# Loads in quarters, and the first group's projections, statistics and norm inside the context phase

## What is computed

```python
x = x + attn(layernorm(x))            # 16 heads of 32, causal
x = x + xattn(layernorm(x), ctx)      # below
x = x + ffn(layernorm(x))             # 8 experts of width 1024, top-p routing

# xattn: 16 heads of 128 in 8 groups; fp8_linear rounds its input to fp8 after a division by a scale
q,  k, v = ln(fp8_linear(h, wq)),  ln(fp8_linear(h, wk)), fp8_linear(h, wv)
core     = gqa(q, k, v)                            # two heads of a group share k and v
qx       = ln(fp8_linear(h, wqx))
kx, vx   = ln(ctx @ wkx), ctx @ wvx
xout     = gqa(qx, kx, vx)
return fp8(cat(core, xout) / smooth) @ wproj * scales
```

## Time and profile before

| what | value |
|---|---|
| three runs | 2502.35, 2497.77, 2496.59 us; median 2497.77 |
| the profiled execution | 2499.1 us, span 2497.3 us, mean granted clock of PE 0.967 |
| PE busy | 2314.2 us, 93% of the span |
| DVE, ACT, POOL busy | 57%, 46%, 46% |
| context phase, prologue, steps, experts (start, about) | 310, 533, 565, 1475 us |
| ACT's loads, landing in the median | w_group 5.1 us (1 MB, x15), w_kv 7.5 us (0.5 MB, x7), kv 6.5 us (1 MB, x16) |

### The profile page before, as it was taken

The page is one execution under the profiler, slowest core; times in us unless marked ns, Lnnn a source line. Parts: engine busy times, 40 slices in busy tenths (PEclk is TensorE's granted clock), DMA queues, the critical chain, the costliest instruction groups (busy, mean ns, idle before and its releaser), DMA issues. The chain is left out here.

```text
span 2497.3 us, 39715 instructions
## 1 busy us (share of the span) xinstructions
PE 2314.2 (93%) x14528; PEld 1305.7 (52%) x14528; DVE 1417.8 (57%) x2920; ACT 1139.2 (46%) x2165; POOL 1150.0 (46%) x1412
## 2 busy tenths in 40 slices
PE   6899798958999989999999849999999999999999
PEld 3566544435666666666666534444444444444444
DVE  5766786327999989899999853222222222222221
ACT  3455475438777878777778721111111111111110
POOL 3422346647787878677775423131313131313131
PEclk9799899979999999999999969999999999999999
DMA  4100022217877787878878742111111111111000
GB/s 150 35 19 18 3 83 85 102 68 154 160 143 155 166 167 138 171 154 157 155 144 166 130 136 101 40 62 44 57 46 54 50 50 54 47 58 43 0 0 34
DMA packets 421569, 224.80 MB, mean 90 GB/s; under 512 B 404400, under 2 KB 404912, under 8 KB 413232
## 3 DMA queue, kind: packets, MB, share of 16 engines
q1 hardware_dynamic: 415952, 186.74, 32.5%
q10 hardware_dynamic: 5472, 36.18, 4.3%
HBM read 103.34 MB, written 18.87 MB: 49 GB/s over the span
## 5 line engine op out<-in xcount | busy, mean ns | idle before, releaser
L1835 ACT ACTIVATE sil<-bank 128x512 f32<-128x512 f32 x128 | 76.4, 597 | 772.5 <-PE bank L299 772.5
L1808 POOL TENSOR_SCALAR hh<-h 128x512 f16<-128x512 f32 x128 | 104.8, 819 | 680.8 <-DVE h L1906 680.8
L1906 DVE TENSOR_TENSOR h<-bank,sil 128x512 f32<-128x512 f32 x128 | 88.6, 692 | 530.6 <-PE bank L299 423.1
L1450 ACT ACTIVATE xprob<-bank,xnm 128x1024 f32<-128x1024 f32 (+1 forms) x240 | 219.9, 916 | 184.1 <-DVE xnm L1538 183.7
L1538 DVE TENSOR_REDUCE xnm<-bank 128x1 f32<-128x512 f32 (+1 forms) x256 | 243.2, 950 | 67.7 <-PE bank L299 66.0
L1550 DVE SCALAR_TENSOR_TENSOR xparts<-xprob,xri,xparts 128x1024 f16<-128x1024 f32 (+1 forms) x240 | 278.3, 1160 | 4.4 <-ACT xparts L1458 4.2
L1458 ACT ACTIVATE xparts<-xprob,xri 128x1024 f16<-128x1024 f32 (+1 forms) x240 | 227.5, 948 | 4.6 <-DMA xpt<-xparts 4.5
L297 PE MATMUL bank<-eXTh,ewh_gate 128*128 128x512 f16 x512 | 194.8, 380 | 3.5 <-DVE ewl_gate L1853 3.5
L298 PE MATMUL bank<-eXTh,ewl_gate 128*128 128x512 f16 x512 | 194.8, 380 | 0.0
L299 PE MATMUL bank<-eXTl,ewh_gate 128*128 128x512 f16 x512 | 194.7, 380 | 0.0
L297 PE MATMUL bank<-eXTh,ewh_up 128*128 128x512 f16 x512 | 194.1, 379 | 0.0
(11 more groups left out here) (264 smaller groups left out, 5949.8 us busy)
## 6 DMA issues: line engine op xcount, KB each, us to landing
xkv<-kv_made ACTq DMA_DIRECT2D x16, 1024.0 KB, 6.5
raw_gate<-in_gate SPq DMA_DIRECT2D x8, 2048.0 KB, 7.9
raw_up<-in_up SPq DMA_DIRECT2D x8, 2048.0 KB, 8.0
raw_down<-in_down SPq DMA_DIRECT2D x8, 2048.0 KB, 7.7
xwraw<-in_w_group ACTq DMA_DIRECT2D x15, 1024.0 KB, 5.1
kv_made<-vst SPq DMA_DIRECT2D x16, 512.0 KB, 4.3
kv_made<-kst SPq DMA_DIRECT2D x16, 512.0 KB, 2.6
kvraw<-in_w_kvx SPq DMA_DIRECT2D x4, 1024.0 KB, 6.4
```

Of the source, the lines that this page charges most:

```text
L1450: act.activation(prob[prob_of(u)][:, 0:L], SC[u % 2][:, 0:L], ACT.Exp, bias=nm[:, u % 4:u % 4 + 1], accum_out=rs[:, u % 4:u % 4 + 1]).then ...
L1808: pool.tensor_scalar(hh[half][:, f, :], h[i % 2][:], 1.0, 1.0, ALU.mult, ALU.mult).then_inc(h_hi, 1)
L1835: act.activation(sil[i % 2][:], bank[:, 2 * (i % 2), :], ACT.Silu, scale=1.0 / WS).then_inc(silu, 1)
L1906: dve.tensor_tensor(h[i % 2][:], bank[:, 2 * (i % 2) + 1, :], sil[i % 2][:], ALU.mult).then_inc(made, 1)
```

## The change

- The buffer of the projected blocks, `qr`, and the value parts of batch 0, `v0`, are allocated before `second_norm` and handed to both phases.
- In the context loop PE runs the six jobs A0 to A3, B0, B1 of step 0 at iterations 31, 33, 35, 37, 39 and 41 (`first_job`), in the free banks 0 and 1. ACT reads them one iteration later (`first_read`), DVE makes their low part and statistics two iterations later (`first_low`). POOL makes rstd and shift ahead of its `deviations(5)` (`first_deviations`) and waits for the result. ACT applies them to the four key blocks at iteration 55, DVE to 16 blocks in iterations 54 to 61, two in each.
- `total` is no buffer of its own any more: DVE writes y + unit over y, and so ACT waits for `r_out`, the end of the last subtraction, before it fills y again. The statistics of the first jobs lie in `unit`. Chain buffers are shared.
- The prologue of the group stage keeps only T_ORDER = T4 T0 T1 T2 T3; counts on semaphores are lowered to match.
- Each load of the group stage becomes four transfers, each a quarter of every partition's row: kv in slots 6 to 9 of both batches, w3 in slots 10 to 13 of b = 0, w2 two by two in slots 4 and 5 of b = 0, w1 of group g + 2 in slots 10 to 13 of b = 1, and w1 of group 1 in slots 0 to 3 of step 0. The first kv load, ahead of the steps, is also in four.

```diff
+FIRST_FROM, FIRST_EVERY = 31, 2
 def second_norm(...):
+    FIRST = ("A0", "A1", "A2", "A3", "B0", "B1")
+    def first_at(i):
+        return [(i - FIRST_FROM) // FIRST_EVERY] if (i >= FIRST_FROM and (i - FIRST_FROM) % FIRST_EVERY == 0
+                                                     and (i - FIRST_FROM) // FIRST_EVERY < len(FIRST)) else []
...
             for q in range(BATCHES):
+                if q == BATCHES - 3:
+                    first_deviations()
+                    pool.wait_ge(f_shift, 1)
                 deviations(q)
...
-                    act.wait_ge(r_dve, ROUND_STEPS * (j - 1))
+                    act.wait_ge(r_out, j - 1)
...
                 read(i)
+                for f in first_at(i - 1):
+                    first_read(f)
+                if i == 55:
+                    act.wait_ge(f_shift, 1)
+                    for k in ACT_APPLIES:
+                        act.activation(first_block(k), first_block(k), ACT.Identity, scale=frstd[:, k:k + 1],
+                                       bias=fshift[:, k:k + 1])
...
-                round_fp8(dve, r_dve, ROUND_STEPS * j, y[j % 2][:], unit[:], total[:])
+                round_fp8(dve, r_dve, ROUND_STEPS * j, y[j % 2][:], unit[:], y[j % 2][:])
...
+                for f in first_at(i - 2):
+                    first_low(f)
+                if 54 <= i < 62:
+                    dve.wait_ge(f_shift, 1)
+                    for k in (2 * (i - 54), 2 * (i - 54) + 1):
+                        dve.tensor_scalar(first_block(k), first_block(k), frstd[:, k:k + 1], fshift[:, k:k + 1],
+                                          ALU.mult, ALU.add)
...
+            def first_job(f):
+                if f == 0:
+                    pe.wait_ge(L_f, B * KT)
+                    pe.wait_ge(r_out, B * KT)
+                if name[0] == "A" and f >= 2:
+                    pe.wait_ge(f_read, f - 1)
...
             for i in range(CROSS):
                 project(i)
+                for f in first_at(i):
+                    first_job(f)
                 for j in norms_at(i):
                     turn_norm(j)
...
 def group_attention(...):
-            deviations(0)
-            apply(0)
             for name in T_ORDER:
                 turned_lo(name, 0, 0)
...
-                    act.dma_start(wraw[:], ins["w_group"][bass.ds(g, 1), chunk // 2].rearrange("a p k n -> p (a k) n"))\
-                        .then_inc(w_in, 16)
+                    act.dma_start(wraw[:, k, :], ins["w_group"][g, chunk // 2, :, k, :]).then_inc(w_in, 16)
...
-            for name in NEXT:
-                if name == "T4":
-                    apply_keys(0)
+            for name in T_ORDER:
                 read_job(name, 0, 0)
...
-                    if b == 0:
-                        if u == 0 and not last_group:
-                            load(1, g + 1, w_base(g))
-                            load(2, g + 1, w_base(g))
-                        if u == 8:
-                            load(3, g, w_base(g) + (W1N if not last_group else 0))
-                            load_kv(g, 1, PAIRS * n)
-                    if b == 1 and u == 8 and not last_group:
-                        load_kv(g + 1, 0, PAIRS * n)
+                    if n == 0 and u < KT:
+                        load(1, 1, 0, u)
+                    if b == 1 and 10 <= u < 10 + KT and g + 2 < GROUPS:
+                        load(1, g + 2, w_base(g + 1), u - 10)
+                    if b == 0 and 6 <= u < 6 + KT:
+                        load_kv(g, 1, PAIRS * n, u - 6)
+                    if b == 0 and 10 <= u < 10 + KT:
+                        load(3, g, w_base(g) + (W1N if not last_group else 0), u - 10)
+                    if b == 1 and 6 <= u < 6 + KT and not last_group:
+                        load_kv(g + 1, 0, PAIRS * n, u - 6)
+                    if b == 0 and u in (4, 5) and not last_group:
+                        for k in (2 * u - 8, 2 * u - 7):
+                            load(2, g + 1, w_base(g), k)
...
-            for name in NEXT:
-                run_job(name, 0, 0, NEXT, ())
+            for name in T_ORDER:
+                run_job(name, 0, 0, T_ORDER, ())
```

## The result

| | before | after |
|---|---|---|
| median of the runs | 2499.53 us (6 runs) | 2487.08 us (6 runs) |
| ratio after to before | | 0.9955, 95% interval 0.994 to 0.997 |
| profiled execution: time / span | 2499.1 / 2497.3 us | 2486.31 / 2484.5 us |

The kernel became 12.45 us faster where 24.5 were forecast: the sign was right, the size about half. Over all executions on record (64 of before with a mean of 2499.6 us, 11 of after with 2485.9) the gain is 13.8 us, give or take 3.1.

What follows compares the result with a forecast made beforehand. PE (TensorE) was taken as the bound, so time is won only where it waits. Terms -25.3 + 10.6 + 1.7 - 12 + 0.5 = -24.5 us gave 2473.3 us, own range 2467 to 2480, 8-in-10 range 2463 to 2488.

Steps and rivals of the forecast that it cites:

- (4): Group stage steps: loads in four pieces stop late transposes and PE's waits for them; -12 us, bounds 0 and -16.
- (1): Group stage prologue: only the chain T4 to T3 remains, first scores after 6.5 us in place of 31.8; -25.3 us.
- (2): Context loop: the six moved jobs run on PE, which has no free time there; +10.6 us, all on the path.
- (3): Context loop: POOL's first_deviations delays the norm of batch 5, so PE waits; +1.7 us, bounds 0 and 3.
- The second way of counting, by steps: Batch 0 steps: five burst steps coming down to 55.3 us give 11.4, the first step perhaps 1.5.
- perhaps 1.5: Step 0 of the group stage: the gain expected from the pieces, in us.
- The statistics come later anyway: Step 0: POOL's first split starts some 3 us later, but its next statistics come later still; counted as nothing.
- Batch 1 steps stay 54.0: Group stage: batch 1 steps keep their length of 54.0 us; longer ones would show the forecast wrong.
- (5): ACT's queue: 114 more issues, 111 in the steps, 0.34 us each; +0.5 us, bounds 0 and 7.
- The pieces bring nothing: Rival, group stage: transposes are held up by bytes, not bursts, and waits only move to other slots; 2485.3 us, chance 0.20.
- more than forecast: Rival, group stage: w1 landed early brings batch 0 steps down to 53.96 us, 9 us more; 2464 us, chance 0.10.
- fixed price per piece: Rival, slots 10 to 13: each piece costs the DMA engines a fixed time; about 2563 us, chance 0.04.

Runs made afterwards that it cites:

- experiment 1: The moved work of the first step alone: the kernel after, with whole loads where they were before; 2491.13 us, ratio 0.9961 to before.
- experiment 8: Kernel after with the six jobs two at a time at iterations 27 to 29, not singly from 31 to 41; 2475.82 us, ratio 0.9904 to before.
- experiment 2: The pieces alone: the kernel before, with the four-piece loads of the kernel after; 2496.55 us, ratio 0.9985 to before.
- experiment 6: Kernel after with the second group's w1 pieces issued ahead of the steps, not in slots 0 to 3 of step 0; 2487.97 us.
- experiment 10: Kernel after with jobs at 27 to 29, POOL's chain behind batch 5's norm, early scalings, w1 pieces two per slot in step 0; 2464.11 us, ratio 0.9854.
- experiment 5: Kernel after with POOL's scalings of raw w1 and w2 ahead of its wait for A3; 2476.86 us, ratio 0.99 to before.
- experiment 11: Kernel with jobs at 27 to 29, POOL's chain later and scalings early, but whole loads in place of pieces; 2467.81 us, ratio 0.9873 to before.
- the best kernel: Kernel after with jobs at 27 to 29, later POOL chain, early scalings, w1 pieces two per slot in step 0; run twice, 2464.11 and 2461.49 us.
- experiment 9: Whole loads as in before, the moved work of the first step, and POOL's scalings ahead of its wait for A3; 2477.64 us, ratio 0.9912 to before.
- 12: Second run of the kernel after with moved jobs, later POOL chain, early scalings and w1 pieces two per slot in step 0; 2461.49 us, ratio 0.984.

## Why the prediction was off by half

The measured 2487.08 us lies outside the forecast's own range of 2467 to 2480, though inside the wide one of 2463 to 2488. The term that failed is (4), the pieces; a chance of the clock hid a further part in the profile.

**(1) Prologue, right.** -25.3 forecast, -24.6 to the first scores. The chain T4 to T3 took 7.15 us and not 6.5: PE's first wait is 1.46 us, since ACT issues four pieces of kv ahead of its first read (0.77 us with the one load of experiment 1).

**(2) Six jobs, right in size, wrong in "all of it on the path".** +10.6 forecast, +10.57 measured, 1.75 us for each A and 1.79 for each B. That PE "has no free time there" was read in the window 420 to 470 alone. The gap of 7.3 us just ahead of it would have taken them all (experiment 8).

**(3) POOL's chain, right.** +1.7 forecast, 1.89 as a wait, 2.1 in the iterations.

**(4) The pieces, wrong.** -12 forecast, -6.7 in the first pair of profiles, -4.8 with three profiles of each kind, -3.7 by the means of experiment 2. The failed step is "the measured price of the bursts is the 12.5 us": it took PE's wait for the transposes as time to be won. The wait did go (12.5 to 1.4 us), but behind it stood the next one. The wait for cat was to "stay near 16" and became 22.8 us, since PE now comes to cat earlier and POOL does not; and 3.8 us for the norm in step 0 took the place of 3.2 for a transpose. The second way of counting, by steps, gave "the same" by luck:
- The six steps of batch 0 were forecast to fall by 11.4 us to 332.0. They fell to 333.5, and to 333.4 in experiment 2. That target was right but for the clock (below). The starting point was not: 343.4 in the profile of before, 338.3 in the second one, 341.3 in experiment 1. I took one execution's delays of single transposes for the kernel's. In the second profile of before the two ways of counting give 11.6 (the wait) and 6.3 us (the steps).
- Step 0, "perhaps 1.5" of gain and "I count nothing" for the late last piece of w1. It took 52.48 us in place of 50.25. POOL's timeline, before and then after:

```profile
577.10 4.07 POOL L1311 TENSOR_SCALAR xwraw<-xwraw,cols 128x256 f32<-128x256 f32 x8 [8.82 <-PE bank L1639]
...
590.75 0.25 POOL L1330 TENSOR_TENSOR xmsum<-xstats 128x20 f32<-128x20 f32 x1 [1.42 <-DVE xstats L1527]
```

```profile
574.11 4.62 POOL L1434 TENSOR_SCALAR xwraw<-xwraw,cols 128x256 f32<-128x256 f32 x8 [12.00 <-DMA xwraw<-in_w_group]
...
586.68 0.24 POOL L1453 TENSOR_TENSOR xmsum<-xstats 128x20 f32<-128x20 f32 x1
```

  The split starts 12.7 us into the step in place of 9.6, as forecast. "The statistics come later anyway" failed: POOL had only 1.42 us to spare ahead of them, so the chain behind the split starts 2.0 us later in the step (25.3 in place of 23.3). With the piece early step 0 takes 49.84 us (experiment 6), with two per slot 48.86 (experiment 10, at full clock throughout). Of PE's wait of 3.8 us for the norm, though, 2.7 stay even then: that part is the overlap above.
- "Batch 1 steps stay 54.0": they take 54.27. So do two of the seven in the profile of before and five of seven in its second one; I had taken the lower of two levels for the only one. 1 us in all.

**(5) Issues, right in the steps.** The steps of batch 1 hold eight pieces and take what they take with one load. At the seam an issue costs its full 0.46 us.

**The rivals.** *The pieces bring nothing* had 2485.3 us, the number nearest to the 2487.08 measured. That is chance: its mechanism, transposes held up by bytes and not by bursts, is refuted by the landings (10.7 to 7.2 us at most) and by the wait for xpt; in the first pair of profiles the half clock took back 5.7 us of the 6.7 that the pieces gave. "POOL waits for A3, not for the load" was my argument against *more than forecast*; the cure was thus not the early load but POOL's order, and it brings what that rival priced at 9 us: 8.7 (810.9 in experiment 5, against 818.2 and 821.1 in the two profiles of after). The *fixed price per piece* did not come: on the page the queue of these loads has a share of 5.6% and not 4.3% of the engines, 32 us in each engine over 114 more pieces, or 0.28 us a piece. Pieces land in 3.3 us and whole loads in 5.1 to 6.5:

```profile
xkv<-kv_made ACTq DMA_DIRECT2D x64, 256.0 KB, 3.3
...
xwraw<-in_w_group ACTq DMA_DIRECT2D x60, 256.0 KB, 3.4
```

So a landing has a part of over 2 us that doesn't shrink with its size (6.5 = f + 4s and 3.3 = f + s give f = 2.2). That is near the 2 us of the Trainium skill, "DMA: Bandwidth & Descriptors", section "Anatomy of one DMA", whose figure is for transfers issued by GpSimd; these are ACT's. The section puts most of it down to the confirmation of the landing. No run here shows that, but the 0.28 us a piece says that most of it is not time of the engines. The page's rule to batch DMAs to at least 1 MiB, section "Bandwidth", is one for the share of peak bandwidth; for this kernel it points the wrong way, since whole loads lose 8.4 us in the steps.

**What I had left out: the clock.** A single profile had set every number. In the four profiles that have full clock from 120 to 290 us the context phase's first projection starts at 309.6 to 310.9 us; in eight of the nine with the half clock it starts at 318.4 to 320.4, in the ninth (experiment 11) at 314.3. So this alone moves the phase by 8 to 10 us in eight of the nine, most of the change's whole effect, and both profiles of before happened to be free of it. With the chance parts averaged, -24.5 + 10.6 + 2.1 - 4.8 = -16.6 us is what the parts say (the steps: three profiles with whole loads have a mean of 824.1, three with pieces 819.3), and -13.8, give or take 3.1, is what the executions say. The last 3 us I can't assign; they are within the interval.

## What to carry to other kernels

Price a removed wait by what stands behind it: 7.2 us less wait for the transposes came with 5.6 us more for cat, and only once POOL was early did nearly all of it arrive. Price a moved job by the whole stage that it moves into, and look for the engine's longest wait in that stage before placing it: 10.6 us of matmuls cost 10.6 us two iterations behind a 7.3 us wait, and nothing ahead of it. In front of a wait that an engine has anyway put all that doesn't need it, and read the queue behind the wait: moving one wait on POOL brought at least as much as the pieces. Ask of every baseline number what a second profile would give; where single executions scatter by 5 us, a level read from one is no more certain than that.

## What I had not expected of the hardware

The granted clock of identical code differs from execution to execution: at 275 to 285 us it is 0.50 in nine profiles of fourteen, within a stretch of 20 to 27 us, and 1.00 in five, with the same activity of PE ahead of it (48.5 and 48.3 of 50 us in the two profiles of the best kernel). Of the five, experiment 9 has a shorter stretch of 6.8 us at half clock from 260 on and starts the context phase at 315.2 us.

A wait of PE can cost more than its length. Ten profiles have one or two stretches of 3.4 us at half clock within steps 1 to 14; each begins within a wait of PE of 1.9 to 2.8 us for cat or xpt, or at most 1.2 us behind its end. In after it is step 4. PE's timeline:

```profile
804.30 0.38 PE L1781 MATMUL bank<-xw3h,cat 128*128 128x512 f16 x1 [2.71 <-POOL cat L1485]
```

And the busy time around it:

```profile
803.00:810.00 7.00, 5.70 (x22) 2.58 (x23) 5.61 (x13) 4.06 (x6) 4.75 (x10) 0.76 0.54 123
```

Such a step takes 56.98 us and not 55.3. In the three profiles without any such wait in steps 1 to 14 (experiments 5, 10 and 12) none of these steps has one. Not every wait brings it: the best kernel with whole loads (experiment 11) has waits of up to 2.7 us there and no such stretch. And of the six waits of 2.3 us and more for cat in steps 2 to 12 of after only the one in step 4 does. So what else it takes is open, but its price of 1.7 us comes on top of the waits.
